# Turning two of four layer-normalised blocks with VectorE's 32x32 transposes and a DRAM round trip, and laying x out by 32 tokens, in a float32 attention and gated linear layer

## The reference

```python
x = x + attn(layernorm(x), w_qkv, w_o)
x = x + ffn(layernorm(x), weight, bias, centroids, assignments)
# attn: 32 query heads, 8 key/value heads, head size 128, causal,
#       bias -slope[head] * sqrt(distance), softmax over keys, then @ w_o
# ffn:  (x @ weight.T + bias), kept only where the token and the row's
#       cluster pass softmax(x @ centroids.T / 0.1) > 0.01
```

## Time and profile before

| | |
|---|---|
| median of 3 runs | 1263.79 us (1263.68 to 1264.32) |
| the profiled execution's own time | 1262.71 us |
| its span | 1261.1 us |
| PE (TensorE matmul) busy | 1243.9 us, 99% |
| DVE (VectorE) / ACT (ScalarE) / POOL (GpSimd) busy | 764.1 / 751.8 / 516.0 us |
| granted TensorE clock | full in all 40 slices |
| unit 1 / unit 2 / 36.5 us of the loop, as windows | PE busy 38.9 of 43.4 / 38.0 of 38.3 / 36.5 of 36.5 us |

### The profile page before, as it was taken

The page is one execution under the profiler, slowest core; times in us unless marked ns, Lnnn a source line. Parts: engine busy times, 40 slices in busy tenths (PEclk is TensorE's granted clock), DMA queues, the critical chain, the costliest instruction groups (busy, mean ns, idle before and its releaser), DMA issues.

```text
span 1261.1 us, 21927 instructions
## 1 busy us (share of the span) xinstructions
PE 1243.9 (99%) x6188; PEld 1051.7 (83%) x6188; DVE 764.1 (61%) x2156; ACT 751.8 (60%) x2154; POOL 516.0 (41%) x476
## 2 busy tenths in 40 slices
PE   8899999999999999999999999999999999999998
PEld 7688888888888888888888888888888888888786
DVE  8877555556555555565555556555555555676777
ACT  3776565666655666666556666665566666655543
POOL 5322636227342555226452364327362274224223
PEclk9999999999999999999999999999999999999999
DMA  6422334334332343424333344323343343422203
GB/s 210 154 92 78 123 117 158 112 104 145 102 128 86 120 143 125 133 100 133 99 125 108 117 149 125 125 91 120 105 150 116 108 150 107 139 68 86 66 17 134
DMA packets 162377, 147.14 MB, mean 117 GB/s; under 512 B 10032, under 2 KB 123696, under 8 KB 162352
## 3 DMA queue, kind: packets, MB, share of 16 engines
q1 hardware_dynamic: 156528, 128.48, 30.5%
q0 software_dynamic: 5824, 18.36, 4.8%
HBM read 84.67 MB, written 62.13 MB: 116 GB/s over the span
## 4 chain that ended last, share of the span: by engine, by line
PE 89%; DVE 5%; ACT 3%; issue 1%; POOL 1%; DMA 1%; SPq 0%; DVEq 0%; ACTq 0%; POOLq 0%
PE ps L1252 84%; PE ps L1331 3%; PE ps L1332 1%; ACT prob L677 1%; ACT prob L686 1%; DVE ring_whole L926 1%; PE ps L1272 1%; DVE stats L847 1%; DVE qT_lo L901 1%; POOL wqkv_lo L480 0%; DVE rs L872 0%; DVE prob L963 0%; DMA acc<-in_L_attn_hidden_states 0%; DVE prob L886 0%; PE ps L1362 0%
## 5 line engine op out<-in xcount | busy, mean ns | idle before, releaser
L1252 PE MATMUL ps<-xnT,wqkv_hi 128*128 (+1 forms) x1568 | 485.3, 391 | 4.8 <-DVE negmax L963 2.8
L523 POOL TENSOR_TENSOR ring<-ring_whole,pT_hi 128x512 fp32r<-128x512 f32 x189 | 244.0, 1291 | 485.1 <-ACT pT_hi L666 484.9
L1252 PEld LDWEIGHTS ps<-xnT,wqkv_hi 128*128 128x128 f32 x1568 | 291.5, 188 | 66.2 <-issue 4.8
L677 ACT ACTIVATE prob<-prob,negmax 128x128 f32<-128x128 f32 (+1 forms) x512 | 226.8, 444 | 180.3 <-DVE negmax L963 179.5
L1252 PE MATMUL ps<-xnT,wqkv_lo 128*128 (+1 forms) x784 | 305.2, 389 | 0.0
L686 ACT ACTIVATE prob<-prob,rinv 128x128 f32<-128x128 f32 (+1 forms) x512 | 190.3, 445 | 62.2 <-DVE rinv L971 62.2
L1252 PE MATMUL ps<-wo_hi,oT_hi 128*128 128x512 f32 x512 | 201.9, 394 | 0.0
L1252 PE MATMUL ps<-wo_lo,oT_hi 128*128 128x512 f32 x512 | 199.8, 390 | 0.0
L1252 PE MATMUL ps<-wo_hi,oT_lo 128*128 128x512 f32 x512 | 199.4, 389 | 0.0
L1252 PEld LDWEIGHTS ps<-xnT,wqkv_lo 128*128 128x128 f32 x784 | 147.2, 188 | 30.7
L943 DVE TENSOR_TENSOR acc<-ps,acc 128x512 f32 (+1 forms) x128 | 88.4, 691 | 127.5 <-PE ps L1252 127.3
(11 more groups left out here) (135 smaller groups left out, 1722.4 us busy)
## 6 DMA issues: line engine op xcount, KB each, us to landing
turned<-ring_whole SPq DMA_DIRECT2D x189, 256.0 KB, 2.1
ring_whole<-turned SPq DMA_DIRECT2D x189, 256.0 KB, 3.0
turned_v<-vT SPq DMA_DIRECT2D x32, 256.0 KB, 2.0
vT<-turned_v SPq DMA_DIRECT2D x31, 256.0 KB, 2.7
raw<-in_L_attn_w_qkv POOLq DMA_DIRECT2D x28, 256.0 KB, 3.1
raw<-in_L_attn_w_o POOLq DMA_DIRECT2D x28, 256.0 KB, 3.2
raw<-in_L_attn_w_qkv POOLq DMA_DIRECT2D x28, 128.0 KB, 3.2
acc<-in_L_attn_hidden_states SPq DMA_DIRECT2D x3, 1024.0 KB, 7.9
```

The lines of the kernel that those rows point to most:

```text
L523: pool.tensor_tensor(ring_slot(c), whole_slot(c), pT_hi[:, c % 2, :].bitcast(F32), ALU.subtract).then_inc(pT_lo_done, 1)
L677: ins = act.activation(s, s, ACT.Exp, bias=negmax[:, n:n + 1], scale=-1.0, accum_out=rowsum[:, n:n + 1])
L1252: ins = pe.matmul(dst, l, r, start=start and m == 0, stop=stop and m == n - 1)
```

## The change

For L = 2 and L = 3 TensorE's transposes go. VectorE applies the normalisation to four tiles in one go into `xw` (the memory of `xnT`, as plain float32), transposes each tile's 32x32 blocks within SBUF, SyncE writes the quad (1 MB) to DRAM and reads it back in four DMAs of 32 partitions each, ScalarE makes the hi part and GpSimd the lo part, both out of SBUF. L = 0, 1 and 4 to 7 keep TensorE's transposes. The free axis of `xnT` of all quads is now tile, block of 32 tokens, chunk, token, so that `project`'s moving operand has 16 runs of 32 elements where it had one of 512. TensorE's wait before `project(1, 2)` is for six score slices now, and `project(2, 2)` has none; the wait before units 2 and 3 is for GpSimd's x_lo. On ScalarE `x_hi` of four tiles stands after `normalise(u, 0)`, and `v_hi_part` goes from before `exps(u, 2)` to behind `exps(u, 4)`. The semaphore counts of the other L are renumbered (`nth`), and `ln_part`, `ln_turned` give the new layout; that is left out below.

```diff
+            def send_x(L):
+
+                sp.wait_ge(x_turned, TPQ * (L - 1))
+                sp.dma_start(turned_x[L], xw[:, L, 0].rearrange("p j x -> p (j x)")).then_inc(x_sent, 16)
+
+            def read_x(L):
+
+                sp.wait_ge(x_sent, 16 * (L - 1))
+                for m in range(P // BLK):
+                    sp.dma_start(xw[m * BLK:(m + 1) * BLK, L, 1].rearrange("p j (a x) -> p j a x", a=P // BLK),
+                                 turned_x[L].rearrange("(a r) (j m x) -> m r j a x", a=P // BLK, j=TPQ,
+                                                       m=P // BLK)[m]).then_inc(x_back, 16)
...
-            with sp.Fori(0, UNITS - 3) as v:
+            turn_v(0)
+            turn_half(0, 0)
+            turn_half(0, 1)
+            for v in range(1, QUADS - 1):
+                send_x(v + 1)
+                read_x(v + 1)
+                turn_v(v)
+                turn_half(v, 0)
+                turn_half(v, 1)
+            with sp.Fori(QUADS - 1, UNITS - 3) as v:
...
+            def x_lo_part(L, j):
+
+                pool.wait_ge(x_hi_done, TPQ * (L - 2) + j + 1)
+                pool.tensor_tensor(xnT[:, L, 1, j, :], xw[:, L, 1, j, :], xnT[:, L, 0, j, :].bitcast(F32),
+                                   ALU.subtract).then_inc(x_lo_done, 1)
...
             for u in range(1, QUADS - 1):
-                plain_body(u)
+                for c in range(CHUNKS):
+                    pT_lo_part(u, c)
+                for j in range(TPQ):
+                    x_lo_part(u + 1, j)
+                v_lo_part(u)
...
+            def x_hi(L, j):
+                act.wait_ge(x_back, 16 * (P // BLK) * (L - 1))
+                act.activation(xnT[:, L, 0, j, :], xw[:, L, 1, j, :], ACT.Copy).then_inc(x_hi_done, 1)
...
-                    else:
+                    elif not by_turn(L):
                         v_hi_part(u)
...
+                        if by_turn(L):
+                            if i == 2:
+                                for j in range(TPQ):
+                                    x_hi(L, j)
+                            elif i == 4:
+                                v_hi_part(u)
...
+            def x_apply(L, j):
+                dve.tensor_scalar(xw[:, L, 1, j, :], acc[:, rows(L, j, 1)], meanvar[:, j, 0:1], rs[:, 5, j:j + 1],
+                                  ALU.subtract, ALU.mult).then_inc(ln_ready, 1)
+
+            def turn_x(L, j):
+                dve.wait_ge(ln_ready, L * TPQ + j + 1)
+                dve.transpose(xw[:, L, 0, j, :].rearrange("p (m c e) -> p c m e", m=P // BLK, e=BLK),
+                              xw[:, L, 1, j, :].rearrange("p (c m e) -> p c m e", c=NC, e=BLK)).then_inc(x_turned, 1)
...
-                    if L is not None:
+                    if by_turn(L):
+                        if i < 2:
+                            ln_stats_of(L, source, 2 * i)
+                            ln_stats_of(L, source, 2 * i + 1)
+                        if i == 1:
+                            ln_var(L)
+                        elif i == 2:
+                            ln_scale(L)
+                            for j in range(TPQ):
+                                x_apply(L, j)
+                        elif 3 <= i <= 4:
+                            turn_x(L, 2 * i - 6)
+                            turn_x(L, 2 * i - 5)
+                    elif L is not None:
...
-                at = [quad_of(u) * (2 * NC * UT) + n * UT for n in range(2 * NC)]
-                terms = [((wqkv_hi[:, c, col:col + D], wqkv_lo[:, c, col:col + D]),
-                          (flat[:, bass.ds(at[c], UT)], flat[:, bass.ds(at[NC + c], UT)])) for c in range(NC)]
+                x_hi, x_lo = [flat[:, bass.ds(quad_of(u) * (2 * NC * UT) + part * (NC * UT), NC * UT)]
+                              .rearrange("p (s c e) -> p c s e", c=NC, e=BLK) for part in range(2)]
+                terms = [((wqkv_hi[:, c, col:col + D], wqkv_lo[:, c, col:col + D]), (x_hi[:, c], x_lo[:, c])) for c in range(NC)]
...
-                        if i == 1 and L is not None:
+                        if i == 1 and L is not None and not by_turn(L):
                             pe.wait_ge(scores_biased, u * SCORE_BANKS)
+                        elif i == 1 and L is not None and u == 1:
+                            pe.wait_ge(scores_biased, len(FIRST_SC) + 1)
...
-                    if L is not None and i >= 4:
+                    if L is not None and i >= 4 and not by_turn(L):
                         ln_transpose(L, 2 * i - 8)
                         ln_transpose(L, 2 * i - 7)
...
-                pe.wait_ge(ln_lo_done, u * TPQ + TPQ)
+                pe.wait_ge(*((ln_lo_done, TPQ + TPQ) if u == 1 else (x_lo_done, TPQ)))
                 body(u, True, True, u + 1, lag=2)
-            pe.wait_ge(ln_lo_done, TPQ * QUADS)
+            pe.wait_ge(x_lo_done, 2 * TPQ)
```

More of the change, by code:

```diff
@@ L68, in build @@
         query_sel = sb("query_sel", [P, 2, TPQ], F32)
+        below = ExitStack()
+        xw = sb("xw", [P, QUADS, 2, TPQ, UT], F32, below)
+        below.close()
         att = ExitStack()
@@ L125, in build @@
         turned_v = nc.dram_tensor("turned_v", [P, UT], F32, kind="Internal").ap()
+        turned_x = {q: nc.dram_tensor(f"turned_x{q}", [P, TPQ * HID], F32, kind="Internal").ap() for q in range(2, QUADS)}
         ps = ctx.enter_context(nc.psum_tensor("ps", [P, 8, 512], F32))
@@ L187, in build @@
         ln_lo_done = sem("ln_lo_done")
+        x_turned = sem("x_turned")
+        x_sent = sem("x_sent")
+        x_back = sem("x_back")
+        x_hi_done = sem("x_hi_done")
+        x_lo_done = sem("x_lo_done")
         ffn_step = sem("ffn_step")
@@ L293, in ffn_x, with by_turn, nth, ln_part @@
             return (x3T_hi, x3T_lo) if p == QUADS - 1 else (x2T_hi, x2T_lo)
-        def ln_part(quad, part, j):
-            if isinstance(quad, int) and quad == LAST:
-                return (x3T_hi, x3T_lo)[part][:, :, j * P:(j + 1) * P]
-            if isinstance(quad, int):
-                return xnT[:, quad, part, :, j * P:(j + 1) * P]
-            flat = xnT[:].rearrange("p q s c t -> p (q s c t)")
-            at = quad * (2 * NC * UT) + part * (NC * UT)
-            return flat[:, bass.ds(at, NC * UT)].rearrange("p (c t) -> p c t", c=NC)[:, :, j * P:(j + 1) * P]
+        def by_turn(L):
+            return L is not None and 2 <= L < QUADS
+        def nth(L):
+            return L if L < 2 else L - 2
+        def ln_part(quad, part, j, L):
+            if L < 2:
+                return xnT[:, quad, part, j, :].rearrange("p (a c e) -> p c a e", c=NC, e=BLK)
+            if quad == LAST:
+                return (x3T_hi, x3T_lo)[part][:, :, j * P:(j + 1) * P]
+            return xnT[:, quad, part, :, j * P:(j + 1) * P]
+        def ln_turned(L, j):
+            bank = ps[:, ln_bank(L, j), :]
+            if L < 2:
+                return bank.rearrange("p (c a e) -> p c a e", c=NC, e=BLK)
+            return bank.rearrange("p (c t) -> p c t", c=NC)
         def score_slices(i):
@@ L415, in turn_half, with send_v, read_v @@
                 turn_in(v, 3 * b + 2)
-            def turn_v(v):
+            def send_v(v):
                 sp.wait_ge(v_turned, v + 1)
                 sp.dma_start(turned_v, vT[:]).then_inc(v_out, 16)
+            def read_v(v):
                 sp.wait_ge(v_out, v * 16 + 16)
@@ L433, in turn_v @@
                                  turned_v.rearrange("(a c) (b x) -> (c b) a x", a=P // BLK, b=P // BLK)).then_inc(v_in, 16)
-            with sp.Fori(0, UNITS - 3) as v:
+            def turn_v(v):
+                send_v(v)
+                read_v(v)
+            turn_v(0)
[8 more added lines that the diff above has]
+            with sp.Fori(QUADS - 1, UNITS - 3) as v:
                 turn_v(v)
@@ L746, in body @@
                             ln_root(L)
-                        if i >= 4:
+                        if i >= 4 and not by_turn(L):
                             ln_hi(L, 2 * i - 8, quad)
@@ L881, in ln_apply @@
                     dve.wait_ge(p_turned, u * CHUNKS)
-                if not (isinstance(L, int) and L == 0):
-                    dve.wait_ge(ln_mm, L * TPQ - TPQ + j + 1)
-                    if j >= PROB_TILES and not (isinstance(L, int) and L >= 6):
-                        dve.wait_ge(ln_mm, L * TPQ + 1)
+                if L > 0:
+                    dve.wait_ge(ln_mm, nth(L) * TPQ - TPQ + j + 1)
+                    if j >= PROB_TILES and L < 6:
+                        dve.wait_ge(ln_mm, nth(L) * TPQ + 1)
                 dve.tensor_scalar(ln_tile(L, j), acc[:, rows(quad, j, 1)], meanvar[:, j, 0:1], rs[:, 5, j:j + 1],
@@ L1269, in ln_transpose @@
                 if not own_banks(L) and j == TPQ - 1:
-                    pe.wait_ge(ln_lo_done, L * TPQ + 1)
+                    pe.wait_ge(ln_lo_done, nth(L) * TPQ + 1)
                 for c in range(NC):
@@ L1414, in body @@
                     pe.wait_ge(qk_lo_done, u * 5 + 5)
-                    if L is not None and attn:
```

(3 more changed lines are left out.)

15 lines of the change are left out of this document (7 added, 8 removed).

## The result

The changed kernel takes **1291.51 us** (median of 4 runs, 1291.35 to 1293.54) against 1264.05 us (4 runs, 1263.68 to 1264.58) for the kernel before, measured with it: a ratio of 1.0217, 95% interval 1.0205 to 1.0228. It is 27.5 us slower. The forecast was 1261.8, within 1259.0 to 1267.0. The profiled execution of the changed kernel took 1291.45 us, with a span of 1289.6.

What follows compares the result with a forecast made beforehand. TensorE, busy 99% of the span at full clock, bounds the kernel; only units 1 and 2 can win. Each wins 1.0 us, layout costs 0: 1262.71 - 1.0 - 1.0 = 1260.7, by the median 1261.8 us, range 1259.0 to 1267.0.

Steps and rivals of the forecast that it cites:

- The layout: Moving operand of project in 16 runs of 32, 2304 matmuls: gaps taken to cost 0; one ns a matmul would be 2.3 us.
- the rival of 2 ns a matmul: Gaps in x slow project's matmuls by 2 ns each, 4.6 us in all, 1266.4 us; chance 0.04.
- The reads: SyncE's four 256 KB reads of x from DRAM: taken as 6.0 us, between 5.3 and 7.9.
- the slower rival: Reads into 32 partitions run at half pace, 8.4 us; x_lo 1.4 late per unit, 1266.6 us; chance 0.22.
- Stops of this length leave the clock alone: TensorE's stops in units 1 and 2: granted clock stays full, as across the 2.84 us wait; no cost.
- x_lo end last: Before units 2 and 3: x_lo ready 5.8 us after x, TensorE waits about 2.2 us, each unit wins 1.0.
- the other path, through scores(1, 7): ScalarE's copies, exps, invert_sums and add_bias before scores(1, 7): about 4.5 us after x is back, shorter than x_lo's 5.8.
- The wait of 2.84 us: TensorE's wait before 47.52 in unit 1: wins 0, as TensorE stands elsewhere as long, for kT_lo and GpSimd, until 54.47.
- The out: SyncE writing the 1 MB quad to DRAM: 4.3 us, as the stores of out take.
- VectorE's row of four applications: VectorE in unit 1, four normalisations then transposes: from 58.99, the fourth transpose ending at 65.43; cost 0.
- The transposes' share: Transposes leaving TensorE: 3.2 us in unit 1 and 2.1 in unit 2, together 5.3 us if nothing replaces them.
- gain = 2 x (7.0 - reads): Units 1 and 2: each us of the reads counts twice; gain no more than 5.3 us, none from 7.0 us of reads.

Runs made afterwards that it cites:

- e1: Kernel before with only the changed layout of x (runs of 32), all transposes still on TensorE, no round trip: 1286.64 us against 1264.06.
- e3: Kernel before, project's six outputs reading x in runs of 512, 256, 128, 64, 32 and 16 elements: 1276.24 us.
- e7: e2 with the four reads of 32 partitions kept, but each row of 8 KB in one piece: 1268.92 us.
- e6: e2 with one read of 128 partitions and 8 KB rows in place of four reads of 32 partitions: 1262.4 us.
- i1: Changed kernel with plain xnT, VectorE transposing every fourth column, one read of 128 partitions in 512 byte pieces per quad: 1271.47 us against 1265.8.
- e2: Changed kernel with project reading xnT in plain order, so the round trip alone: 1271.42 us, ratio 1.006 to the kernel before.
- i2: i1 with the normalising instruction writing columns in block order and each quad going out and back in two halves: 1261.36 us against 1264.44.
- e8: Kernel before, project's operands as 8 runs of 64, one run 1, 2, 0 or 16 elements off, and 16 runs of 32: 1277.1 us.
- e9: Kernel before, project's operands as one run 0, 4, 8, 32 or 24 elements off, and four runs of 128 each 1 off: 1278.64 us.

## Why the prediction was wrong

**The layout: this step failed, and it holds three quarters of the error (22.6 of 29.7 us).** The term was put at 0, and e1 measured 22.6. The forecast wrote "One gap costs nothing that shows; 15 could cost up to the rounding, a few ns. I take 0", and gave the rival of 2 ns a matmul 4 in 100. The row that it argued from, a score slice with two runs of 128 elements, was sound but could not tell: runs of 128 are free in e3 as well. What costs is a run under 64 elements, 10 ns a matmul. The error was to carry a price per gap from runs of 128 to runs of 32, and to leave a term out of the range that is multiplied by 2304 and for which no row of the trace had the shape. At 2304 matmuls "a few ns" is the largest number of the whole sum; 3 ns would have been 6.9 us, outside the whole range.

**The reads: half pace, as the slower rival said, for half of its reason.** It gave 8.4 us, and 8.6 was measured; the forecast took 6.0 from a load of 128 partitions in packets of 2 KB. The Trainium skill's page "SBUF — State Buffer", section "Door 1: The DMA port swizzle", which the prediction quoted, spoke against that row with 189 against 328 GB/s, and e7 against e6 (7.5 against 5.5 us) agrees. Of the 3.1 us between these reads and e6's, e6, e7 and i1 put about 1.1 to 1.4 on the small pieces and 1.7 to 2.0 on the 32 partitions and their four DMAs. The rival had put the whole of its 3.1 over 5.3 us on the partitions, so its near hit was in part luck.

**What the late reads cost: the clock failed.** The rival priced itself at 2 x 1.4 = 2.8 us. In e2 units 1 to 3 cost 5.0: 1.9 by the waits and 3.1 by the clock, which the sum did not have. The step was "Stops of this length leave the clock alone: the granted clock stayed full across the wait of 2.84 us". The same wait went either way. Windows of TensorE over the 4 us behind it, first in the kernel before, then in e3, where it was of 2.81 us:

```profile
47.52:51.52 4.00, 4.00 (x18) 1.00 0.49 137
```

```profile
49.86:53.86 4.00, 4.00 (x11) 0.57 0.47 136
```

In e6 the clock is 0.57 over the 4 us behind a wait of only 1.27. So one row with the clock full was no proof, and the length of a wait does not decide by itself. What does was not found.

**In the changed kernel the chains met elsewhere.** The forecast had x_lo end last. Before unit 2 it was the other path, through scores(1, 7), with its 3.40 us of wait and score slices at the lower clock behind it. Before unit 3 TensorE stopped twice, as forecast (1.00 and 0.83). Against e1 units 1 and 2 are 2.3 us longer, 1.4 of them the clock.

**What was right.** The wait of 2.84 us was worth nothing: it came back as 1.27 and 1.29 at the two places that the prediction named. The out took 3.9 us against 4.3. VectorE's row of four applications to the fourth transpose's end takes 6.11 us (60.51 to 66.62) against 6.44; it ends 1.2 later than the 65.4 of the forecast because unit 1 began 1.45 later. From x's return to x_lo are 5.7 us (79.17 to 84.85) against 5.8, and to scores(1, 7) 4.5, as forecast. v came back at about 82.9, later than the 79 of the forecast, and TensorE shows no wait for it. The transposes' share was about right too: 5.3 us gross were forecast, and i2, where x is in time, keeps 3.5 by unit 3 with 1.2 of waits for x_lo left. The forecast's own formula, gain = 2 x (7.0 - reads), gives -3.2 for 8.6, where e2's waits cost 1.9; the form of the path was right, and the layout and the clock were missing beside it.

## What to carry to other kernels

When a change touches the shape of an operand that thousands of matmuls read, the price of that shape is the first term to bound, and if no row has the shape, the range must hold several ns times the count. Lay out a moving operand of fp32 so that every run begins on a multiple of 256 bytes and is a multiple of 256 bytes long. A transfer whose SBUF side is split into slices of 32 partitions is better rewritten as one of 128, if need be by choosing which columns a block takes; here that, with two halves and adjacent columns for the transposes, turned a loss of 7 us (e2) into a gain of 3 (i2). And compare where in the profile a difference lies before giving it to the change: 3 to 4 of the 28.5 us lay where nothing had been changed.

## What the runs showed of the hardware

- A matmul of 512 columns whose moving operand lies in runs of 32 fp32 values starts 0.2367 us after the one before instead of 0.227 (e1, e3); in runs of 16, 0.2400 (e3); in runs of 64 or more from a multiple of 64, no difference.
- One unbroken run pays 2.5 to 8 ns for a start that is not a multiple of 64 elements; four runs, each one element off, pay 14 ns together (e8, e9).
- 1 MB from DRAM into four slices of 32 partitions took 8.6 us (512 byte pieces) or 7.5 (8 KB); into 128 partitions 6.9 or 5.5 (e2, e7, i1, e6).
- SyncE's queue is taken for 2.71 us by four DMAs of 32 partitions in pieces of 512 bytes, 1.73 by four with rows of 8 KB, 0.33 by one of 128 partitions with rows of 8 KB.
- VectorE's transpose of 128x512 from every fourth column takes 1.05 us against 0.65 from adjacent ones (i1); four normalisations with a strided output take 2.63 against 1.92 us (i2).
- The granted clock of the 4 us from 84 to 88 us, behind a wait of TensorE of 3.40 us, was 0.65, with matmuls of 512 columns 0.43 us apart. Behind waits of 1.27 (e6) and 2.81 us (e3) it was 0.57 over 4 us, behind one of 2.84 (before) 1.00. Near the end it fell without a long wait just before it: 0.76 over 1256 to 1270 us of the changed kernel, after 21 us (1240 to 1261) of which TensorE was busy 20.89 at the full clock. What decides was not found.
